# The opening of an AdaLN attention and mixture kernel: SiLU first, modulation as rows, halves per block, neighbour column at the last tap

## The reference

```python
mod = (silu(c) @ wmod).reshape(2, 6, 1, 512)        # wmod is 512 x 3072
sa, ca, ga, sb, cb, gb = (mod[:, i] for i in range(6))
ga, gb = sign(ga) * max(|ga|, 0.25), the same of gb
h = layernorm(x) * (1 + ca) + sa
# attention: conv over 3 taps (512 -> 3*128), q k v projections to 16 heads of 64,
# causal softmax inside blocks of 128 rows, output projection, projection to 512
x = x + ga * attention(h)
h = layernorm(x) * (1 + cb) + sb
# ffn: base 512x512 + bias, low rank 64, router over 16 experts, top 2, sum of 16 expert deltas
x = x + gb * ffn(h)
```

## Time and profile before

| | us |
|---|---|
| median of 3 runs (lowest, highest) | 516.9 (514.59, 518.91) |
| the profiled execution, its own time | 516.02 |
| its span, first to last instruction | 513.9 |
| TensorE busy | 459.9 |
| VectorE busy | 354.7 |
| ScalarE busy | 301.1 |
| GpSimd busy | 275.1 |

### The profile page before, as it was taken

The page is one execution under the profiler, slowest core; times in us unless marked ns, Lnnn a source line. Parts: engine busy times, 40 slices in busy tenths (PEclk is TensorE's granted clock), DMA queues, the critical chain, the costliest instruction groups (busy, mean ns, idle before and its releaser), DMA issues.

```text
span 513.9 us, 11180 instructions
## 1 busy us (share of the span) xinstructions
PE 459.9 (89%) x4203; PEld 309.2 (60%) x4232; DVE 354.7 (69%) x665; ACT 301.1 (59%) x958; POOL 275.1 (54%) x303
## 2 busy tenths in 40 slices
PE   0979999998999998999999999999999998966676
PEld 0968669564867774767476657757675574442322
DVE  3245687796899889878996795778767767536120
ACT  1051463585898895777757785777877574621110
POOL 5301015531344586387864875673696778586521
PEclk9998996998999999999999999999999999989789
DMA  7499242095256567466473758454575738660441
GB/s 308 81 376 385 92 84 42 2 316 96 46 96 124 129 144 205 85 135 133 102 121 80 134 105 160 96 105 109 106 135 82 145 103 124 103 144 23 82 102 42
DMA packets 144998, 65.31 MB, mean 127 GB/s; under 512 B 134704, under 2 KB 134960, under 8 KB 144560
## 3 DMA queue, kind: packets, MB, share of 16 engines
q1 hardware_dynamic: 144800, 64.57, 55.0%
q10 hardware_dynamic: 144, 0.02, 0.0%
HBM read 26.82 MB, written 4.19 MB: 60 GB/s over the span
## 4 chain that ended last, share of the span: by engine, by line
PE 56%; DVE 11%; POOL 10%; DMA 8%; issue 8%; ACT 4%; SPq 2%; POOLq 0%; ACTq 0%; DVEq 0%
PE C L1000 14%; PE F L921 11%; PE C L921 11%; PE WB L1058 3%; DMA h<-h 3%; PE S L1041 3%; PE WB L957 3%; DMA gT<-g 2%; PE S L966 2%; PE F L957 2%; PE WB L921 2%; POOL oh L565 2%; POOL h L549 2%; SPq L426 2%; POOL G L572 2%
## 5 line engine op out<-in xcount | busy, mean ns | idle before, releaser
L1000 PE MATMUL C<-hT,cw 128*128 128x256 f16 x864 | 105.9, 279 | 3.2 <-DVE cw L789 3.1
L655 ACT ACTIVATE prob<-S,nms 128x128 f32<-128x128 f32 x256 | 89.9, 377 | 14.8 <-DVE p L836 14.1
L1000 PEld LDWEIGHTS C<-hT,cw 128*128 128x128 f16 x864 | 84.3, 100 | 18.9 <-issue 3.4
L541 POOL TENSOR_TENSOR prob<-prob,rinv 128x1024 f32<-128x1024 f32 x32 | 61.5, 1921 | 57.0 <-DVE rinv L841 55.7
L921 PE MATMUL F<-btw,gT 128*128 128x512 f16 x384 | 86.6, 382 | 3.1 <-DMA gT<-g 3.0
L626 ACT ACTIVATE qk<-C,bqk 128x256 f16<-128x256 f32 x128 | 52.7, 478 | 31.7 <-PE C L921 31.2
L921 PEld LDWEIGHTS F<-btw,gT 128*128 128x128 f16 x384 | 37.4, 98 | 47.9 <-DMA gT<-g 4.3
L816 DVE SCALAR_TENSOR_TENSOR qk<-C,bqk,qk 128x256 f16<-128x256 f32 x128 | 54.6, 475 | 9.8 <-ACT qk L626 9.3
L655 ACT ACTIVATION_READ_ACCUMULATOR prob<-S,nms 128x1 f32 x256 | 55.5, 217 | 0.0
L921 PE MATMUL C<-cv,pw 128*128 128x256 f16 x384 | 51.3, 275 | 1.1 <-DVE cv L807 0.6
L921 PE MATMUL F<-bsw,h 128*128 128x512 f16 x192 | 45.4, 387 | 7.0 <-DVE ob L915 7.0
(11 more groups left out here) (149 smaller groups left out, 790.3 us busy)
## 6 DMA issues: line engine op xcount, KB each, us to landing
xa<-in_x_dram SPq DMA_DIRECT2D x8, 512.0 KB, 5.1
xb<-in_x_dram SPq DMA_DIRECT2D x8, 512.0 KB, 4.4
out_dram<-xb SPq DMA_DIRECT2D x16, 256.0 KB, 2.4
wmb<-in_wmod_dram SPq DMA_DIRECT2D x1, 3072.0 KB, 19.0
cw_raw<-in_cw_dram SPq DMA_DIRECT2D x3, 768.0 KB, 6.5
raw<-in_cw_dram SPq DMA_DIRECT2D x3, 768.0 KB, 5.3
wma<-in_wmod_dram SPq DMA_DIRECT2D x4, 512.0 KB, 6.9
bt_raw<-in_btw_dram SPq DMA_DIRECT2D x2, 1024.0 KB, 8.5
```

What stands on the lines that cost most here:

```text
L541: nc.gpsimd.tensor_tensor(prob[:], prob[:], rinv[:, i % 2].unsqueeze(2).broadcast_to([P, 8, P]), ALU.mult).then_inc(p_normal, 1)
L655: ins = nc.scalar.activation(prob[:, h], S[i % len(S)][h // 4][:, (h % 4) * P:(h % 4 + 1) * P], ACT.Exp, bias=nms[:, i % 2, h:h + 1], scal ...
L1000: ins = nc.tensor.matmul(bank_c[:, 0:CH], cw[:, i, a, c, tap, :], hT[:, j % 2, b, c, OWN - 1 + tap:OWN - 1 + tap + CH], start=step == 0, s ...
```

## The change

What it does, part by part:

- **SiLU.** On DVE `sil` stands behind the statistics of chunk 0 and ahead of its normalisation; on ACT it stands ahead of `hs:0:0`.
- **Modulation as rows.** `row:0:0` makes sa and ca as two rows, four pairs of matmuls with 512 moving columns, one pair for each of the four loads as it lands, into two PSUM banks. DVE copies both rows to `row_ab`, and `cols:0:0` is now eight TensorE transposes of 2 x 128 pieces. `row:0:3`, `row:0:4` and `cols:0:1` do the same for sb and cb. `fbias` is made once as a row for both batches, multiplied by gb as a row, and spread by two more `pick` matmuls.
- **Halves per block.** `hs` and `hs2` are done for each block of 128 rows by itself: ACT's high half, the low half, and the transpose, with a semaphore for each block (`h_moved[b]`). For chunks 0 and 1 the low half of `hs` is made by DVE instead of POOL.
- **Neighbour column.** The convolution runs tap by tap (all of tap 0, then 1, then 2) instead of channel by channel. Its first matmul waits for its own chunk; the column of the next chunk is awaited at step 24 of the first third, the first of the last tap.
- **Loads.** The other two thirds of the convolution weight and the three projection weights are issued by ACT behind `hs:0:0`. SP issues x of chunks 2 and 3 ahead of the other weights. The ffn bias is loaded as two rows instead of 128.
- **The list.** `SCHEDULE` is another list from end to end: all stages stand in another order to each other.

The diff, cut to its core:

```diff
     SCHEDULE = """
-        na:0:0 nb:0:0 hs:0:0 sil:0:0 na:1:0 nb:1:0 halo:0:0 hs:1:0 halo:1:0 cols:0:0 vb:0:0 sp:0:0 c:0:9 sp:0:1
...
+        halo:0:0 na:0:0 sil:0:0 nb:0:0 na:1:0 hs:0:0 row:0:0 nb:1:0 cols:0:0 hs:1:0 halo:1:0 sp:0:0 sp:0:2 sp:0:1
...
+        s:2:1 lr:0:0 c:3:15 sp:0:11 e:2:0 gbb:0:0 ra:0:1 ro:0:0 nz:2:0 m:2:1 c:3:3 nb:5:0 c:3:21 rw:0:0 c:3:3 G:0:0
...
@@ SP
                 if s == "hs":
-                    sp.wait_ge(h_lo, j + 1)
...
                     for b in range(2):
+                        sp.wait_ge(h_lo, 2 * j + b + 1)
                         sp.dma_start_transpose(
                             hT[:, j % 2, :, :, OWN + b * P:OWN + (b + 1) * P].rearrange("p m c q -> p (m c) q"),
-                            h16[:, b].rearrange("p m d -> p (m d)")).then_inc(h_moved, 16)
+                            h16[:, b].rearrange("p m d -> p (m d)")).then_inc(h_moved[b], 16)
                     if j == 1:
-                        for n in range(1, 3):
-                            sp.dma_start(cw_raw[:, n], cw_in[:, n]).then_inc(ld[f"cw{n}"], 16)
-                        for n in range(3):
-                            sp.dma_start(pw_raw[:, n], pw_in[:, n]).then_inc(ld[f"pw{n}"], 16)
+                        for i in range(2):
+                            sp.dma_start(xa[:, i], xin[i + 2]).then_inc(ld_xa[i], 16)
@@ GpSimd
                 elif s == "hs":
-                    pool.wait_ge(h_hi, j + 1)
-                    nc.gpsimd.tensor_tensor(h16[:, :, LO], xa[:, j % 2], h16[:, :, HI], ALU.subtract).then_inc(h_lo, 1)
+                    for b in range(2 if j > 1 else 0):
+                        pool.wait_ge(h_hi, 2 * j + b + 1)
+                        nc.gpsimd.tensor_tensor(h16[:, b, LO], xa[:, j % 2, b], h16[:, b, HI], ALU.subtract
+                                                ).then_inc(h_lo, 1)
@@ ScalarE
                 elif s == "hs":
-                    act.wait_ge(xn_ready, 2 * j + 2)
-                    if j > 0:
-                        act.wait_ge(h_moved, 32 * j)
-                    nc.scalar.activation(h16[:, :, HI], xa[:, j % 2], ACT.Copy).then_inc(h_hi, 1)
+                    for b in range(2):
+                        act.wait_ge(xn_ready, 2 * j + b + 1)
+                        if j > 0:
+                            act.wait_ge(h_moved[b], 16 * j)
+                        nc.scalar.activation(h16[:, b, HI], xa[:, j % 2, b], ACT.Copy).then_inc(h_hi, 1)
+                    if j == 0:
+
+                        for n in range(1, 3):
+                            act.dma_start(cw_raw[:, n], cw_in[:, n]).then_inc(ld[f"cw{n}"], 16)
+                        for n in range(3):
+                            act.dma_start(pw_raw[:, n], pw_in[:, n]).then_inc(ld[f"pw{n}"], 16)
@@ VectorE
+                elif s == "hs" and j < 2:
+                    for b in range(2):
+                        dve.wait_ge(h_hi, 2 * j + b + 1)
+                        nc.vector.tensor_tensor(h16[:, b, LO], xa[:, j, b], h16[:, b, HI], ALU.subtract).then_inc(h_lo, 1)
                 elif s == "fbias":
-                    link(nc.vector.tensor_tensor(gbBB[:, n], m_bank(stage)[:], bbB[:], ALU.add))
...
+                    link(nc.vector.tensor_tensor(fb_row[:], m_bank(stage)[0:NB, :], bb_row[:], ALU.add))
+                    nc.vector.tensor_tensor(fb_row[:], fb_row[:], gb_row[:], ALU.mult).then_inc(m_done, 1)
@@ TensorE
                     for k in range(DC):
+                        if n == 0:
+
+                            pe.wait_ge(ld[f"wma{k}"], 16)
+                            nc.tensor.matmul(S[0][1][0:NB, :], silT[:, 0, k * NB:(k + 1) * NB], held[:, k, 1, :],
+                                             start=k == 0, stop=k == DC - 1)
                         ins = nc.tensor.matmul(m_bank(stage)[0:NB, :], silT[:, 0, k * NB:(k + 1) * NB], held[:, k, n % 3, :],
                                                start=k == 0, stop=k == DC - 1)
...
                 elif s == "cols":
...
                     for m in range(2):
-                        for c in range(DC):
-                            at = (m * DC + c) * NB
-                            for k in range(DC):
...
+                        for k in range(DC):
+                            at = (m * DC + k) * NB
+                            ins = nc.tensor.transpose(m_bank(stage)[:, at:at + NB], row_ab[:, m, k * P:(k + 1) * P],
+                                                      pick[:, :, 0])
...
                 elif s == "c":
                     i, step = n
+                    tap, c, (a, b) = step // (3 * DC), step // 3 % DC, PASSES[step % 3]
...
-                            pe.wait_ge(h_ready, H_DONE[min(j + 1, NCH - 1)])
+                            pe.wait_ge(h_ready, H_DONE[j] - (1 if j == NCH - 1 else 0))
+                            for moved in h_moved:
+                                pe.wait_ge(moved, 16 * (j + 1))
...
-                    c, tap, (a, b) = step // (3 * TAPS), step // 3 % TAPS, PASSES[step % 3]
+                    if step == 2 * 3 * DC and i == 0:
+
+                        pe.wait_ge(h_ready, H_DONE[min(j + 1, NCH - 1)])
```

More of the change, by code:

```diff
@@ L284, in bass_adaln_block @@
         out_stored = [sem(f"out_stored{i}") for i in range(2)]
[L285 removed]
+        h_moved, h2_moved = ([sem(f"{n}{i}") for i in range(2)] for n in ("h_moved", "h2_moved"))
         c_full, c_done = ([sem(f"{n}{i}") for i in range(len(C))] for n in ("c_full", "c_done"))
@@ L978, in _ @@
                     pe.wait_ge(pool_chain, N_CONST)
-                    pe.wait_ge(m_done, max(mod_by(("row", 2)) if n < 2 else mod_by(("row", 5)), m_before(stage)))
-                    nc.tensor.matmul(m_bank(stage)[:], pick[:, n % 2, :], (ga_row if n < 2 else gb_row)[:], start=True, stop=True).then_inc(m_full, 1)
+                    of, rows = [(("row", 2), ga_row), (("row", 5), gb_row), (("fbias", 0), fb_row)][n // 2]
+                    pe.wait_ge(m_done, max(mod_by(of), m_before(stage)))
+                    nc.tensor.matmul(m_bank(stage)[:], pick[:, n % 2, :], rows[:], start=True, stop=True).then_inc(m_full, 1)
                 elif s == "bias":
```

181 lines of the change are left out of this document (94 added, 87 removed).

## The result

| | before | after |
|---|---|---|
| median (lowest, highest) | 516.88 (514.29, 519.17), 16 runs | 519.5 (516.2, 521.79), 16 runs |
| ratio, 95% interval | | 1.0052 [1.0027, 1.0077] |
| the profiled execution, its own time | 516.02 | 517.92 |
| its span | 513.9 | 516.1 |

The forecast was 499 and its range ended at 509. The change gave nothing; it cost 0.5%.

The account below looks back on a forecast made before the run. TensorE was taken to bound the kernel from 36 to 450 us, but not at its ends. Opening 10.9, second modulation and ffn bias 4.5 and halves 2 sum to 17.4 off 516.02: 498.6, said as 499, range 490 to 509.

Parts of the forecast that it names:

- the columns: Opening: the first modulation's columns, made from rows by eight TensorE transposes, ready at 20.1 us against 27.7 before.
- the bias products' end: Opening: two bias products, 48 narrow instructions ahead of the convolution, take 9.3 us and are done at 29.5.
- The sum of work: TensorE's 72 convolution matmuls, three bias products, one row and six projection matmuls done at 46.2 against 57.1: gain 10.9 us.
- The split of the first third: Opening: VectorE's split of the convolution weight's first third, done at about 23.5 us, hidden behind the bias products.
- the case of the full clock held through: Opening: bias products end at 26.0 us, sum of work at 41.1, gain 16.0; in the 489 us rival, chance 0.11.
- the low-clock case: Opening: rows at the low clock throughout, columns at 26.3 us, gain 3.6; the 507 us rival, chance 0.20.
- The second modulation: Two rows, 7.2 us, and transposes, 1.5, replace 10.05 and a slow stretch: gain 3.2; with the ffn bias 4.5.
- that sign: End of the kernel: the last transposes into `h2` landing 35 us before the end would show the forecast right.
- Then the same work in another order: Opening, behind the bias products: convolution, third bias product, row and projection matmuls end at 46.2 us; gain 10.9.
- The new list gives most of it back in the middle: Rival: TensorE's idle time in the middle rises from 14.4 to about 27 us; 512 to 521, chance 0.08.
- The slower rival: Convolution weight reloads hold SP and ScalarE's exponentials 9 us each, three for 27; 526 if all reach TensorE; chance 0.06.
- the bound of 20: Wrong if TensorE idles over 20 us between the opening and the last chunk.

Follow-up runs that it names:

- early_reload: The kernel after, with SP issuing pending reloads of the residual's x ahead of hs, hs2 and gh transposes too; 504.3 us.
- warm_start: early_reload plus unneeded work on TensorE: 24 wide matmuls until about the first load's landing and two spare row matmuls behind the rows; 502.4 us.
- silu_late: early_reload with the SiLU back in its old place, behind chunk 0's normalisation and halves; 510.3 us.
- loads_on_sp: early_reload with the loads of the other two convolution weight thirds and the projection weights on SP again, behind chunk 1's transposes; 509.9 us.
- old_halves: The kernel before with only the halves per block of 128 rows, low halves on GpSimd, list untouched; 512.6 us.
- first_wait: early_reload with the neighbour column awaited at a chunk's first convolution matmul again, order of the taps kept; 521.7 us.
- open_best: warm_start with the split of the convolution weight's first third ahead of chunk 1's halves in the list; 498.4 us, three runs.

## Why the prediction was wrong, step by step

**Right.** TensorE's first instruction (7.5 said, 7.70), the columns (20.1, 19.5), the bias products' end (29.5, 30.0). Two errors cancel up to there: the transposes were costed at 1.5 us and took 0.62; the bias products were to run fast until 21.7 and ran at the slow pace from their start. The sum of work, 72 convolution matmuls included, was said for 46.2 and came at 47.9, because 15 convolution matmuls behind the third bias product took 3.28 us where 1.7 was said: behind that narrow product the clock was low as well (granted 0.61 and 0.54 in the two stretches of 2 us from 36). In early_reload's trace, with the same opening, the sum came at 46.3, so the size of this term changes by 1.6 us from one execution to another. The split of the first third, said for 23.5, began on VectorE only at 25.70, as ScalarE stood in its wait for chunk 0's transposes until 22.2; the slow bias products hid that. For the same reason the case of the full clock held through, with the convolution at 26.0, could not have come: warm_start's waits for the split until 27.85. In the low-clock case the columns come at 25.3 by its own terms, and 26.3 is said; no chance hangs on it. silu_late gives the SiLU's share as 5.9 (6.0 said), loads_on_sp the loads' as 5.5 (4 said), old_halves that of the halves as 3.1 (2 said; 1.9 to 4.3 by its interval). The second modulation took 3.60, 3.60 and 0.65 us, with no stretch at the low clock before 110, as said. The last `h2` landed 35 us before the end, but it did so in before too (479.17 of 513.9), so that sign could tell nothing.

**The step that failed** is the one behind "Then the same work in another order": the gain of the opening was carried unchanged to the end, because TensorE idled 14.4 us of 355 in the old list. That number is a property of the old order. I costed the new list at nothing but its three weight reloads, and never followed the other load that SP issues out of the list's order, `load_again`, whose place depends on the next `ph`. It was not in the rows and not in the sum. Its price is 15.2 us (early_reload), three quarters of the gap of 20.5 between 499 and 519.5.

**The rivals.** "The new list gives most of it back in the middle" was what happened, at 0.08, but without a mechanism it could not be weighed. The slower rival had the right queue and the wrong load: `ra:0:1` and `ra:0:2` waited 2.0 us in sum in the trace after, where I had 9 for each:

```profile
SPq L434 <- DVE cw L807: 2.0, 2, 1.2
```

The idle time of 23.1 us between 95 and 450 passed the bound of 20 at which I said that I would be wrong.

**The neighbour column** was costed at nothing, from the opening. Under the old list no new wait shows. Under the new one, which starts four of the chunks ahead of the next chunk's `halo`, it is worth 17 us. The list uses what the edit allows, and the two can't be costed apart.

**What is left.** With the reload mended, 504.3 stands against 499. At `wo` of chunk 7 it leads by 9.4 us, where the terms of the opening and the second modulation sum to 15.4; from there to the first product of the last `h2` (467.72, before 479.17) it gains 2.0 more, as said for the halves. So 6 us are lost in between, and from 95 to 450 TensorE idles 20.4 us against 14.4 before, at a granted clock of 0.98 against 1.00. Which of its waits (2.4 us at 108, 2.2 at 144, 3.0 at 387, 3.6 at 430) could go was tried for the first alone, without success.

## What to carry to other kernels

When a change rewrites the order of the work, list every action whose place in a queue is not written but follows from another stage (a deferred load, a store), and look up for each what stands ahead of it in the new order. A low idle share of the bounding engine says that the old order hid the waits, not that a new one will. Put a load that frees a buffer where its wait ends, not on the back of a stage that may move; and when a relaxed wait looks worthless, ask whether the order now leans on it.

## What the runs showed of the hardware

- **A short wait can cost more than itself.** Behind TensorE's wait of 2.43 us in early_reload, 12 convolution matmuls take 2.14 us, where 24 take 2.80 at the full clock (after, at 97.2); the granted clock from 100 to 120 is 0.91. Not every wait does it: behind one of 2.13 us in first_wait 18 take 2.14, the full pace. In first_wait 10.6 us of added waits cost 17. I had costed waits at their length alone.
- **The pace of the same work differs between executions.** The same 48 narrow instructions behind the same rows took 10.37 us in after's trace and 7.84 in early_reload's; behind spare wide work they took 6.97 (warm_start) and 8.37 (open_best). The 24 convolution matmuls that follow took 4.31, 4.95, 4.39 and 4.82: the clock that one part wins the next may lose.
- **Transposes on TensorE are cheap**: eight float32 ones of 2 x 128 took 0.62 us together (after), beside 13.81 for the column form.
